# The last batch's sum over the scan states moved from POOL into two PSUM banks, with new lists for the two last passes

## What is computed

```
x = x + attention(layernorm(x))        # 16 heads of 8, ratio of two score matrices
x = x + moe_ffn(layernorm(x))          # 8 experts, top 2, and a shared one, exact gelu
x = x + mamba(layernorm(x))            # 256 inner channels, 16 states
x = x + moe_ffn(layernorm(x))          # the same weights
```

```
h_s[t] = exp(dt[t]*A_s) * h_s[t-1] + dt[t]*x[t]*B_s[t]
y[t]   = sum over the 16 states of h_s[t] * C_s[t]
```

## Time and profile before

| what | value |
|---|---|
| time, median of 3 runs | 3860.93 us (3859.01, 3860.93, 3870.79) |
| the profiled execution | 3871.34 us, its span 3869.4 us |
| PE / DVE / ACT / POOL busy over the span | 89% / 71% / 84% / 33% |
| POOL yM, L1330 | 240 operations, 595.1 us, mean 2479 ns |
| DVE scan, dbx, hc (L1222, L1218, L1229) | mean 2487, 1478, 1289 ns |
| mean granted TensorE clock | 0.943 of full speed |

### The profile page before, as it was taken

The page is one execution under the profiler, slowest core; times in us unless marked ns, Lnnn a source line. Parts: engine busy times, 40 slices in busy tenths (PEclk is TensorE's granted clock), DMA queues, the critical chain, the costliest instruction groups (busy, mean ns, idle before and its releaser), DMA issues. The chain is left out here.

```text
span 3869.4 us, 38405 instructions
## 1 busy us (share of the span) xinstructions
...
## 2 busy tenths in 40 slices
...
GB/s 147 46 136 61 117 123 184 143 148 160 121 174 131 176 138 178 152 122 195 116 185 123 179 148 140 168 122 175 142 169 133 185 145 134 179 99 160 122 127 101
DMA packets 214848, 552.02 MB, mean 143 GB/s; under 512 B 25105, under 2 KB 96626, under 8 KB 214642
## 3 DMA queue, kind: packets, MB, share of 16 engines
...
## 5 line engine op out<-in xcount | busy, mean ns | idle before, releaser
L783 PE MATMUL bank<-hF,wst 128*128 128x512 f32 x2304 | 1171.9, 625 | 25.3 <-DVE tmp L1180 20.8
L1110 DVE TENSOR_TENSOR rPool<-bank,rPool 128x512 f32<-128x512 f32 x1024 | 703.1, 687 | 559.7 <-PE bank L713 514.1
L885 ACT ACTIVATE hF<-bank,cols 128x512 f32<-128x512 f32 x1152 | 770.9, 686 | 253.9 <-PE bank L774 245.5
L1330 POOL TENSOR_TENSOR yM<-yM,ws 128x1024 f32<-128x1024 f32 x240 | 595.1, 2479 | 1026.1 <-DVE ws L1229 1023.7
L1023 ACT ACT_TABLE_LOAD x554 | 710.8, 1283 | 9.7
L885 ACT ACTIVATE rPool<-bank 128x512 f32<-128x512 f32 x1024 | 571.2, 596 | 162.4 <-PE bank L708 156.9
L772 PE MATMUL bank<-xnH,wst 128*128 128x512 f32 x1152 | 599.5, 520 | 68.5 <-DMA wst<-wscr 36.4
L1222 DVE TENSOR_TENSOR_SCAN ws<-dAs,ws 128x1024 f32<-128x1024 f32 x256 | 635.5, 2487 | 6.9 <-ACT dAs L885 5.5
L1315 POOL TENSOR_TENSOR acc<-acc,tmp 128x512 f32<-128x512 f32 x240 | 353.1, 1471 | 835.7 <-DVE tmp L1180 827.3
L783 PEld LDWEIGHTS bank<-hF,wst 128*128 128x128 f32 x2304 | 412.7, 193 | 434.4 <-issue 347.7
L713 PE MATMUL bank<-qpk,kpk 48*128 48x512 bf16 x1024 | 420.3, 410 | 122.6 <-DVE rPool L1110 122.0
...
## 6 DMA issues: line engine op xcount, KB each, us to landing
wst<-wscr SPq DMA_DIRECT2D x288, 768.0 KB, 5.5
bc<-bcscr SPq DMA_DIRECT2D x256, 512.0 KB, 4.9
cB<-gscr SPq DMA_DIRECT2D x256, 256.0 KB, 4.8
...
kpk<-kscr SPq DMA_DIRECT2D x128, 192.0 KB, 6.0
qpk<-qscr SPq DMA_DIRECT2D x128, 192.0 KB, 6.5
wscr<-wst SPq DMA_DIRECT2D x9, 512.0 KB, 2.9
```

The lines of the kernel that those rows point to most:

```text
L783: pe.matmul(ps[FFN][:, :], w2, hF[:, (NCH * f + q) % HSLOTS, :], start=(c == 0), stop=(c == FC - 1)).then_inc(s_dn, 1)
L885: return nc.scalar.activation(out_, in_, fn, **kw)
L1110: v.tensor_tensor(rP[:, slot, c, :], ps[NUM][:, :], rP[:, slot, c, :], ALU.mult).then_inc(s_mul, 1)
L1330: g.tensor_tensor(yM[:, :, :], yM[:, :, :], ws[:, s % 3, :, :], ALU.add).then_inc(s_ya, 1)
```

## The change

The scan of batch 15, the last one, is summed on PE. The identity matrix is the stationary operand and the two halves of ws are streamed into banks 0 and 1, accumulating over the 16 states. ACT then copies the banks into yM (`E.take`). The 15 M.acc of the LAST list are gone, `hc` of state 0 writes ws and not yM, and `dbx` waits for PE's sum of state s-3 (s_ysum). Both passes have new lists on all engines. Of the lists those of LAST on PE, DVE (its second half) and POOL are shown whole, of the others only what changes place:

```diff
 LAST = {
     "SP": """
...
-    F.gate*2 F.w F.gate F.w F.gate F.w G.w F.gate G.w*3 M.rows G.rows G.gate*2 M.bc*5 G.w M.bc*2 G.gate*2 G.w M.bc*2
-    G.w*2 M.bc G.gate M.bc G.gate*2 M.bc*2 G.w G.gate M.bc*3 G.out
+    N.bc F.w F.gate*3 G.w*4 G.rows G.gate G.w G.gate*2 G.w G.gate*2 G.w G.gate G.w G.gate G.w M.rows M.bc*7 G.gate
+    M.bc*4 G.out M.bc*5
     "PE": """
-    H.down F.mean H.down*3 H.up*4 H.down*4 H.up*2 H.down F.var H.down*3 H.up*4 F.router H.down*4 F.up*3 H.close F.up
-    F.down F.turn F.down F.up*4 F.down*4 F.up F.down*2 F.up*6 F.down*4 F.up*4 F.down*4 F.up*3 F.down*4 F.up*6 F.down
-    E.mean F.down*3 E.var F.down*2 F.up F.down F.up F.down F.up*2 E.gate F.up*2 G.mean F.down F.up G.var F.up
-    F.down*3 G.router G.up F.down*4 G.turn G.up*2 M.mean G.up M.var G.down*2 M.ip*2 G.down M.ip G.up*2 G.down M.ip
-    M.ss G.up M.dt G.down G.up M.dt G.down*3 G.up*3 G.down*3 G.up*3 G.down G.up*2 G.down G.up*2 G.down*5 G.up*5
-    G.down*2 G.up G.down G.up*4 G.down*5 G.up*2 G.down*2 G.up*4 G.down*4 G.up G.down G.up G.down*3 G.close
+    H.up*4 H.down*3 H.up H.down F.mean H.down*4 H.up*2 H.down F.var H.up*2 H.down*3 H.up F.router H.down*2 F.up
+    H.down*2 F.up*2 H.close F.up F.turn F.down F.up*2 F.down*3 F.up F.down F.up*3 F.down F.up F.down*2 F.up*3 F.down
+    F.up F.down*4 F.up F.down*3 F.up*2 F.down*2 F.up*5 F.down F.up*2 F.down*5 F.up*5 F.down*5 F.up*2 F.down E.mean
+    F.up F.down*2 E.var F.up*2 F.down*3 F.up E.gate F.down G.mean G.var G.router G.up*4 G.down*2 G.up*2 G.down*2
+    G.up G.turn G.up*2 M.mean G.down*2 G.up*4 G.down*2 G.up G.down*2 G.up*2 G.down M.var G.up G.down G.up*2 G.down*4
+    G.up*2 G.down*2 M.ip G.down*2 M.ip G.up*2 M.ip*2 G.up*2 G.down*3 M.ss G.down M.dt G.up*2 G.down G.up G.down G.up
+    M.dt G.down*2 G.up*2 M.sum G.up G.down M.sum G.up*3 M.sum*2 G.up G.down M.sum G.down*3 M.sum G.down*3 G.close
+    M.sum*10
     "ACT": """
...
+    M.decay*2 T.gelu G.gelu*2 T.log M.decay T.gelu G.gelu*2 T.log M.decay T.gelu G.gelu*2 T.silu M.silu T.log
+    M.decay*4 G.close M.decay*6
     "DVE": """
...
-    F.part G.turn M.mean M.var M.conv*8 G.part*2 M.dt M.dbx M.scan M.hc M.dbx M.scan M.hc M.dbx M.scan M.hc M.dbx
-    M.scan M.dbx M.hc M.scan G.part M.hc M.dbx M.scan M.hc M.dbx G.part M.scan M.dbx M.hc M.scan G.part M.hc M.dbx
-    M.scan M.dbx M.hc G.part M.scan M.hc M.dbx M.scan M.dbx M.hc M.scan G.part M.hc M.dbx M.scan M.hc M.dbx G.part
-    M.scan M.dbx M.hc M.scan G.part M.dbx M.scan M.hc*2
+    N.scan N.hc*2 F.part E.mean F.part E.var E.gate F.part G.mean G.var G.router G.route G.turn G.part M.mean
+    G.part*3 M.var M.conv G.part M.conv*7 G.part*2 M.dt M.dbx M.scan M.hc M.dbx M.scan M.hc M.dbx M.scan M.hc M.dbx
+    M.scan M.hc M.dbx M.scan M.hc M.dbx M.scan M.hc G.part M.dbx M.scan M.dbx M.hc M.scan G.part M.hc M.dbx M.scan
+    M.hc M.dbx M.scan M.dbx M.hc M.scan M.hc M.dbx M.scan M.hc M.dbx M.scan M.hc M.dbx M.scan M.hc M.dbx M.scan M.hc
+    M.dbx M.scan M.hc
     "POOL": """
-    N.acc H.add*4 N.acc*6 F.add*2 N.acc*2 F.add*5 M.take G.add M.acc*5 G.add M.acc*2 G.add M.acc*2 G.add M.acc*2
-    G.add M.acc G.add M.acc G.add*2 M.acc*2 M.keep
+    H.add*3 N.acc H.add N.acc*3 F.add*2 N.acc*3 F.add*2 N.acc*2 F.add*3 M.take M.keep G.add*8
 END = {
     "ACT": """
-    E.mean E.var G.mean G.var T.gelu G.gelu*4 T.log G.router T.gelu G.gelu*32 G.close T.log
+    E.take E.mean E.var G.mean G.var T.gelu G.gelu*4 T.log G.router T.gelu G.gelu*32 G.close T.log
...
         @block.tensor
+                elif name == "sum":
+                    if n == 0:
+                        pe.wait_ge(s_ln, UNITS * NB)
+                    pe.wait_ge(s_hc, NS * m + n + 1)
+                    for h in range(2):
+                        mm = pe.matmul(ps[h][:, :], ident[:, :], ws[:, n % 3, h, :], start=(n == 0), stop=(n == NS - 1))
+                    mm.then_inc(s_ysum, 1)
             def scan_norm(m, i, name):
                 if name == "mean":
-                    pe.wait_ge(s_ya, floor((NS - 1) * (m + 1)))
+                    if m == NB - 1:
+                        pe.wait_ge(s_ytake, 2)
+                    else:
+                        pe.wait_ge(s_ya, floor((NS - 1) * (m + 1)))
         @block.scalar
             def scan_norm(m, name):
-                if name == "mean":
+                if name == "take":
+                    act.wait_ge(s_ysum, NS)
+                    act.wait_ge(s_E_proj, m)
+                    for h in range(2):
+                        a(yM[:, h, :], ps[h][:, :], ACT.Copy).then_inc(s_ytake, 1)
+                elif name == "mean":
         @block.vector
-                    if s >= 3:
+                    if s >= 3 and m == NB - 1:
+                        v.wait_ge(s_ysum, s - 2)
+                    elif s >= 3:
                         v.wait_ge(s_ya, floor((NS - 1) * m + s - 3))
...
-                    if s == 0:
+                    if s == 0 and m < NB - 1:
                         v.wait_ge(s_E_proj, floor(m))
-                    dst = yM[:, :, :] if s == 0 else w
+                    dst = yM[:, :, :] if s == 0 and m < NB - 1 else w
```

More of the change, by code:

```diff
@@ L178 @@
     "SP": """
-    N.bc*2 H.gate N.bc H.w F.w H.gate N.bc F.w*2 H.out N.bc*2 F.w F.rows F.gate N.bc F.gate*2 F.w N.bc*2 F.w
-    F.gate*2 F.w F.gate F.w F.gate F.w G.w F.gate G.w*3 M.rows G.rows G.gate*2 M.bc*5 G.w M.bc*2 G.gate*2 G.w M.bc*2
-    G.w*2 M.bc G.gate M.bc G.gate*2 M.bc*2 G.w G.gate M.bc*3 G.out
+    N.bc*2 H.w H.gate*2 F.w N.bc F.w N.bc F.w F.rows F.w F.gate*2 N.bc*2 F.gate*2 F.w N.bc*2 F.w*2 F.gate H.out F.w
+    N.bc F.w F.gate*3 G.w*4 G.rows G.gate G.w G.gate*2 G.w G.gate*2 G.w G.gate G.w G.gate G.w M.rows M.bc*7 G.gate
@@ L190 @@
+    F.up F.down*2 E.var F.up*2 F.down*3 F.up E.gate F.down G.mean G.var G.router G.up*4 G.down*2 G.up*2 G.down*2
[3 more added lines that the diff above has]
+    M.sum*10
 """,
     "ACT": """
-    N.decay*2 T.gelu H.gelu*6 F.mean T.log N.decay T.gelu H.gelu*2 T.log F.var T.gelu H.gelu*4 T.log F.router T.gelu
@@ L193 @@
[L193 to L197, removed]
@@ L198 @@
-    M.decay*2 T.gelu G.gelu*5 T.log M.decay T.gelu G.gelu T.log M.decay T.gelu G.gelu*2 T.log M.decay T.gelu
-    G.gelu*3 T.log M.decay T.silu M.silu T.gelu G.gelu*2 T.log M.decay T.gelu G.gelu T.log M.decay G.close
+    T.gelu H.gelu*7 T.log N.decay T.gelu H.gelu*2 F.mean T.log F.var N.decay T.gelu H.gelu*3 F.gelu*2 T.log F.router
+    T.gelu F.gelu H.close F.gelu*2 T.log N.decay*2 T.gelu F.gelu*8 T.log N.decay*2 T.gelu F.gelu T.log N.decay
+    T.gelu F.gelu*11 T.log N.decay*2 T.gelu F.gelu*8 E.mean T.log E.var T.gelu F.gelu*3 G.mean T.log G.var T.gelu
@@ L200 @@
+    G.gelu*4 T.log G.router T.gelu G.gelu*7 M.mean G.gelu*8 T.log M.var T.gelu G.gelu*2 M.xp*2 G.gelu*2 M.xp*2
+    T.silu M.silu*3 T.gelu G.gelu M.row G.gelu*3 M.dt G.gelu M.dt T.log M.sp M.decay*2 T.gelu G.gelu*2 T.log
+    M.decay*2 T.gelu G.gelu*2 T.log M.decay T.gelu G.gelu*2 T.log M.decay T.gelu G.gelu*2 T.silu M.silu T.log
+    M.decay*4 G.close M.decay*6
 """,
     "DVE": """
-    F.mean N.dbx H.part N.scan N.hc N.dbx H.part N.scan N.dbx N.hc H.part F.var F.router N.dbx H.part N.scan F.route
@@ L203 @@
-    N.hc N.scan F.turn N.hc N.dbx F.part N.scan N.dbx N.hc N.scan F.part N.hc N.dbx N.scan N.hc F.part N.dbx N.scan
-    F.part N.dbx N.hc N.scan F.part N.hc E.mean F.part E.var F.part E.gate G.mean G.var F.part G.router G.route
-    F.part G.turn M.mean M.var M.conv*8 G.part*2 M.dt M.dbx M.scan M.hc M.dbx M.scan M.hc M.dbx M.scan M.hc M.dbx
-    M.scan M.dbx M.hc M.scan G.part M.hc M.dbx M.scan M.hc M.dbx G.part M.scan M.dbx M.hc M.scan G.part M.hc M.dbx
-    M.scan M.dbx M.hc G.part M.scan M.hc M.dbx M.scan M.dbx M.hc M.scan G.part M.hc M.dbx M.scan M.hc M.dbx G.part
@@ L208 @@
-    M.scan M.dbx M.hc M.scan G.part M.dbx M.scan M.hc*2
+    H.part F.mean H.part N.dbx*2 N.scan*2 F.var H.part N.hc F.router H.part F.route N.hc N.dbx F.turn N.dbx F.part
+    N.scan*2 N.hc*2 F.part N.dbx*2 F.part N.scan*2 N.hc*2 F.part N.dbx N.scan N.hc N.dbx F.part N.scan N.dbx F.part
+    N.scan N.hc*2 F.part E.mean F.part E.var E.gate F.part G.mean G.var G.router G.route G.turn G.part M.mean
+    G.part*3 M.var M.conv G.part M.conv*7 G.part*2 M.dt M.dbx M.scan M.hc M.dbx M.scan M.hc M.dbx M.scan M.hc M.dbx
```

11 lines of the change are left out of this document (7 added, 4 removed).

## The result

The changed kernel takes 3871.0 us (median of 20 runs, 3858.1 to 3883.3), the kernel before 3859.5 (20 runs, 3851.4 to 3870.8). The ratio is 1.0025, 95% interval 1.0014 to 1.0037: 0.25% slower. The interval excludes 1, so the change is real, and it lies within the 0.3% that I called no change. The forecast was 3867.9, +7.0; the medians lie 11.5 apart, the ratio stands for 9.7.

The account below looks back on a forecast made before the run. It took DVE's scan of batch 15, with POOL's adds on its path, and PE in FFN 31 as the bounds. Terms -24.0 + 28.0 + 3.0 + 0.5 - 0.5 = +7.0 on 3860.93 gave 3867.9 us, range 3853 to 3881.

Parts of the forecast that it names:

- Part 1: Scan of batch 15: POOL's adds of yM gone, 83.9 against 107.9 us, -24.0 (bounds -27 and -17).
- Part 2: PE ahead of the scan, first G.up to M.dt2: more G.up and G.down there, +28.0 us (bounds +24.5 and +34).
- Part 3: Norm of batch 14: more F.part and F.add ahead of it, +3.0 us (-1 to +7); the norm itself +0.5.
- Part 4: From M.dt2 to the first dbx: same operations, 7.5 us, row loads hidden, change 0 (to +1).
- Part 5: Tail from last hc to the mean: last sum and two copies, 4.2 against 4.7 us, -0.5 (-1.6 to +0.1).
- Part 6: END: same work in another interleaving, PE bound, change 0 us (-1 to +1).
- A: Rival: PE's added work ahead of the scan fits into its waits, -16 us, 3845; chance 0.08.
- B: Rival: tightly packed, all low bounds that can meet, -2.5 us, 3858; chance 0.17.
- C: Rival: PE stays at half clock in the scan and DVE waits for it, +18 us, 3879; chance 0.27.
- the cold entry: Within C: PE also enters the work ahead of the scan at a low clock, +4 us.
- the marks that I named: Signs of being right, among them first dbx of batch 15 near 3697, last hc near 3781, PE over 90% busy ahead of M.dt.

Follow-up runs that it names:

- e1: Kernel before with the new lists, the sum of batch 15 left on POOL; 3896.2 us, ratio 1.0092 against the kernel before.
- e3: Changed kernel with the lists of LAST up to G.router put back to the old ones; 3860.3 us, ratio 0.9994 against the kernel before.
- e4: Sums on PE, new lists of LAST up to G.router, old ones from there on; 3870.7 us, ratio 1.0021 against the kernel before.
- e2: Kernel before with its old lists, the sums moved to PE, some PE chunks reordered; 3851.8 us, ratio 0.9974 against the kernel before.
- e7: Changed kernel with the norm of batch 14 placed earlier, among the FFN 29 chunks as before; 3871.3 us, ratio 1.0031 against the kernel before.
- e13: Changed kernel with first-half DVE and ACT lists reordered to take out DVE's waits; 3873.0 us, ratio 1.0023 against the kernel before.
- e14: e13 with a row ahead of a weight on SP, and ACT decays and a DVE scan earlier; 3866.4 us, ratio 1.0010 against the kernel before.

## Why the prediction was right, point by point

- *What bounds.* Right. POOL was on the path of the scan; with its adds gone the chain stays on DVE, and e1 against the changed kernel gives the size, 105.6 against 80.5. The Trainium skill (SBUF — State Buffer, "SBUF: two separate sides") calls DVE's and GpSimd's shared port pair an exclusive lock held for a whole instruction; the rows agree, a scan took 2.29 alone against 3.17 beside a G.add and 4.32 beside an add of yM.
- *Part 1, scan: -24.0 forecast, -27.4 measured.* The 80.9 of DVE work was 80.5, a wait of 1.1 for rows in it. The 3.0 for PE holding DVE was nothing. Both G.add within the scan collided, which makes 2 and not 3; they cost a scan 0.9 (3.17) and a dbx 1.1.
- *Part 2, front: +28.0 forecast, +28.5 or +28.6 measured* (58.4 to 58.5 against 29.9). The sum is right by luck, its make-up is not: PE was busy 57.6 of 58.5, where I had 53.4 and 4.5 of waits. The error stood in my own rows: I priced the work before at 20.7 and called the other 9.2 waits, while the earlier trace rows has PE busy 26.0 of 29.9, idle for 3.9. I kept 4.5 of waits; PE was idle for 0.9, and work of 4.2 more than I had priced stood in their place. The first four G.up ran with starts 0.43 apart and not 0.23, half clock, for some 2.4 us more (12 x 0.2), which is more than half of those 4.2.
- *Part 3, the norm of batch 14: +3.0 forecast with bounds -1 and +7, +12.3 measured.* This term failed, and lies outside its bounds. I priced it by work (two F.part, two F.add, one collision), and DVE's work did not grow, it fell from 76.8 to 70.4; the loss is in DVE's waits, 22.7 in place of 5.1 in the rows above. My sentence that FFN 29 is hidden because PE has 71 busy of 84.9 was wrong in kind: the busy share tells nothing of the order in which DVE waits for it. The norm itself: +0.5 forecast, 22.7 or 22.8 against 23.5.
- *Part 4*: 0 forecast, 7.4 against 7.4 (the 7.3 and 7.5 of the rows are rounding). *Part 5, tail*: -0.5 forecast, 4.7 against 4.7; the last sum ran at half clock (3.44), the mean at full (1.98), where before it was 3.39. *Part 6, END*: 0 forecast, 92.9 against 91.7, no more than END differs between profiles with the same END lists (e3 90.4, changed 92.9). In END only the lists of SP, PE and ACT are new. The table loads fell by fifteen as counted (555 to 540).
- *The sum*: +7.0 forecast. By stretches of this pair it is +13.8: 12.3 + 28.5 - 0.8 - 27.4 + 1.2. The 20 runs give 9.7 to 11.5. So the scan was priced 3.4 too dear and the stretch ahead of the norm 9.3 too cheap, and the total is near partly because these have opposite signs.
- *Rivals.* A is out: PE took the added work in one piece. B is out: the scan and the norm (22.7) passed their low bounds, but the front (+28.5 against +24.5) and the stretch ahead of the norm did not come near theirs. C, half clock throughout the scan: its mean clock was 0.84, DVE never waited for PE, so it didn't happen; the cold entry (+2.4) and a last sum at half clock are what came of it. Of the marks that I named, the first dbx came at 3691.1, the last hc ended at 3771.6. Both look early against my 3697 and 3781, but that execution ran 14 us ahead; with these added they are 3705 and 3786, 8 and 5 late, because the norm of batch 14 came 12.3 late and not 3.0. Counted from that norm the first dbx is 27.7 later than before.

What stays open: which of the edits in the first half costs the 12 to 14 us. Shown are its place (the same in e1, e4 and the changed kernel, gone in e2 and e3), that it isn't the number of chunks ahead of the norm (e7), and that waits taken out return, in part as other waits and in part as DVE operations lengthened by POOL's adds (e13, e14). That it is the whole ring of parts, gelus, decays and rows, slower by its order, is what remains, but it is argued, not shown. No run puts PE's or ACT's first half back alone.
